# Four half steps moved and a norm rebalanced in a seven-stage attention kernel

## The reference

```
L0: y = norm(x + attention(x, x, causal)), lengths taken from the scores   a0
    y = norm(y + attention(y, ctx))                                        a1
    x = norm(y + relu(y W1 + b1) W2 + b2)            width 256             f0
L1: x = x + attention(rms(x), rms(x), mask) Wo                             a2
    x = x + attention(rms(x), ctx, mask) Wo                                a3
    x = x + mixture of 8 experts, top 2, and a shared one                  moe
L2: the same two attentions with biases and layer norms, then              a4 a5
    x = norm(x + relu(x W1 + b1) W2 + b2)            width 1024            f2
L3: out = norm(x + attention(x, ctx, causal)) * gamma + beta, 8 heads      a6
```

## Time and profile before

| | us |
|---|---|
| runs shown | 2715.59, 2716.20, 2718.04; median 2716.2 |
| profiled execution, its own time | 2713.54 |
| its span | 2711.2 |
| mean granted TensorE clock | 0.961 |

### The profile page before, as it was taken

The page is one execution under the profiler, slowest core; times in us unless marked ns, Lnnn a source line. Parts: engine busy times, 40 slices in busy tenths (PEclk is TensorE's granted clock), DMA queues, the critical chain, the costliest instruction groups (busy, mean ns, idle before and its releaser), DMA issues. The chain is left out here.

```text
span 2711.2 us, 44385 instructions
## 1 busy us (share of the span) xinstructions
PE 2493.1 (92%) x16014; PEld 1367.7 (50%) x16014; DVE 1770.2 (65%) x4316; ACT 1402.3 (52%) x1969; POOL 750.9 (28%) x915
## 2 busy tenths in 40 slices
PE   6999998989999999997999998799999999797896
PEld 3544433333444434443999998334434443385553
DVE  3566777677666676774457774577777777455554
ACT  1555565555555555555348875155555555452332
POOL 2244434443321111101016564202222112223012
PEclk7999999999999999998899999699999999998998
DMA  5222222122223223220127885423322322001331
GB/s 169 60 52 72 58 62 64 37 65 53 56 80 108 64 73 92 73 53 20 44 82 217 223 220 125 125 64 85 103 67 71 94 69 65 3 8 40 84 85 41
DMA packets 102213, 218.55 MB, mean 81 GB/s; under 512 B 19116, under 2 KB 35372, under 8 KB 100716
## 3 DMA queue, kind: packets, MB, share of 16 engines
q1 hardware_dynamic: 93164, 203.66, 27.8%
q0 software_dynamic: 8832, 12.06, 2.3%
HBM read 100.34 MB, written 12.58 MB: 42 GB/s over the span
## 5 line engine op out<-in xcount | busy, mean ns | idle before, releaser
L1150 ACT ACTIVATE probT_a<-scores 128x1024 f32<-128x1024 f32 (+3 forms) x832 | 779.3, 947 | 696.1 <-PE scores L981 422.6
L1265 DVE CUSTOM_DVE_ANT_0 ring<-ring,maskb_a 128x512 f32<-128x512 f32 x1024 | 686.3, 716 | 186.9 <-PE ring L999 177.6
L999 PE MATMUL ring<-stacks_a 64*128 64x512 f32 (+7 forms) x1664 | 465.2, 458 | 60.3 <-DVE negm_a L1263 24.4
L1020 PE MATMUL outputs<-probT_a,V_a 128*32 128x512 f32 (+6 forms) x3328 | 441.6, 574 | 12.3 <-ACT oT_a L1159 8.3
L1263 DVE TENSOR_REDUCE negm_a<-ring 128x1 f32<-128x512 f32 (+3 forms) x640 | 331.5, 564 | 152.1 <-PE ring L1005 110.4
L999 PEld LDWEIGHTS ring<-stacks_a 64*128 64x128 f32 (+1 forms) x1664 | 207.6, 189 | 381.0 <-issue 139.4
L960 PE MATMUL scores<-stacks_a 64*128 64x512 f32 (+7 forms) x1664 | 392.3, 444 | 2.5 <-DMA stacks_a<-narrow_a 2.5
L960 PEld LDWEIGHTS scores<-stacks_a 64*128 64x128 f32 (+1 forms) x1664 | 167.8, 185 | 241.9 <-issue 156.0
L909 POOL TENSOR_SCALAR maskb_a<-ints_a 128x1024 bf16<-128x1024 int32 x31 | 112.9, 3641 | 385.8 <-DMA ints_a<-in_mask 290.9
L981 PE MATMUL scores<-maskT_a,identb 64*64 64x512 bf16 x1024 | 210.2, 401 | 0.0
L981 PE MATMUL scores<-swapped_a,identb 64*64 64x512 bf16 x1024 | 206.8, 401 | 0.0
(11 more groups left out here) (243 smaller groups left out, 3760.7 us busy)
## 6 DMA issues: line engine op xcount, KB each, us to landing
stacks_a<-parts_a SPq DMA_DIRECT2D x672, 128.0 KB
raw<-in_moew SPq DMA_DIRECT2D x92, 512.0 KB, 4.1
ints_a<-in_mask SPq DMA_DIRECT2D x31, 512.0 KB, 3.7
swapped_a<-maskT_a SPq DMA_DIRECT2D x32, 256.0 KB, 3.6
wt<-in_w SPq DMA_DIRECT2D x7, 1024.0 KB, 4.9
kvT_a<-in_ctxT SPq DMA_DIRECT2D x12, 512.0 KB, 3.4
wrow<-in_row SPq DMA_DIRECT2D x7, 512.0 KB, 5.8
stacks_a<-narrow_a SPq DMA_DIRECT2D x224, 8.0 KB
```

The source lines that it names most:

```text
L999: last = pe.matmul(bank("S", j, n, e)[:, 0:w], Q[rows, g, qt * P:(qt + 1) * P], K[rows, g, 0:w], start=True, stop=not a.causal)
L1020: last = pe.matmul(OB[x * slot:(x + 1) * slot, q0:S], V[:, m % 2, kb, c:c + slot], probT[:, kb % 2, x, q0:S], start=(kb == 0), stop=(kb == ...
L1150: act.activation(probT[:, kb % 2, 2 * p:2 * p + 2, q0:S], scores_bank(j, n)[:, :, q0:S], ACT.Exp, bias=0.0, scale=-1.0).then_inc(c_exp.sem, 1)
L1265: least = dve.tensor_tensor_reduce(sc, sc, maskb[:, m % 2, qt, :], 1.0, BIG * 2, ALU.add, ALU.min, out)
```

## The change

- In the table: "q" part 1 of the next unit in a0 and a1 from half step 9 to 8; "tokens" from 18 to 17 (to 16 for a stage on the context with rms norm, a3), "norms" from 21 to 19 (a3: 20); the second "fh" from 17 to 16.
- In L3 a new flag `apart` holds: "root" is issued with "on", "ln" two half steps after "on"; POOL forms `shift` as well, and ACT centres instead of DVE.
- The last unit of L3 gets its gain and bias on DVE instead of POOL.
- Each batch's output leaves in two transfers of two tiles.
- `schedule` is rewritten with an inner function; the order of the list that it gives for a given table is the same.

```diff
+        self.apart = self.spaced or dk == 32
@@ timetable
         if a.spaced:
             out += [(2 + t, "root", -1, qt), (5 + t, "ln", -1, qt)]
+        elif a.apart:
+            out += [(2 + t, "root", -1, qt), (4 + t, "ln", -1, qt)]
         else:
             out += [(t + (5 if a.wo else 3), "root", -1, qt), (t + (5 if a.wo else 3), "ln", -1, qt)]
...
-    out += [(h + 1, "q", 1, 1), (h + 3 if a.length else h + 2 * step, "k", 1, 1), (2 * h + 1, "V", 1, 0), (2 * h + 2 * step, "V", 1, 1)]
+    out += [(h if a.length else h + 1, "q", 1, 1), (h + 3 if a.length else h + 2 * step, "k", 1, 1), (2 * h + 1, "V", 1, 0), (2 * h + 2 * step, "V", 1, 1)]
...
-    out += [(2 * h, "cnld", 2, 0), (2 * h + step, "tokens", 2, 0),
-            (2 * h + 5 * step // 2, "norms", 2, 0),
+    out += [(2 * h, "cnld", 2, 0), (2 * h + (0 if a.kv == "ctx" else step // 2), "tokens", 2, 0),
+            (2 * h + (4 if a.kv == "ctx" else 3) * step // 2, "norms", 2, 0),
...
-    out += [(13, "fx", -1, 0), (14, "fx", -1, 1), (15, "fh", -1, 0), (17, "fh", -1, 1)]
+    out += [(13, "fx", -1, 0), (14, "fx", -1, 1), (15, "fh", -1, 0), (16, "fh", -1, 1)]
@@ sync
-                if kind == "ln" and last and n == QT - 1:
+                if kind == "ln" and last and n % 2 == 1:
                     _, b, _, _ = stage_of(j)
-                    for t in range(QT):
+                    for t in range(n - 1, n + 1):
                         sp.wait_ge(*c_done.at(j, t))
-                    sp.dma_start(io["out"][b:b + 1, :, :].rearrange("o (q p) d -> p (o q) d", p=P),
-                                 X[:, b * QT:(b + 1) * QT, :]).then_inc(c_out.sem, 16)
+                    sp.dma_start(io["out"][b:b + 1, (n - 1) * P:(n + 1) * P, :].rearrange("o (q p) d -> p (o q) d", p=P),
+                                 X[:, b * QT + n - 1:b * QT + n + 1, :]).then_inc(c_out.sem, 16)
@@ gpsimd
-                    if a.spaced or kind == "froot":
+                    if a.apart or kind == "froot":
...
+                    if last_unit(j):
+                        continue
                     pool.wait_ge(*c_centred.at(*key))
@@ scalar
-                if kind == "fl" or (kind == "ln" and att[units[j][0]].spaced):
+                if kind == "fl" or (kind == "ln" and att[units[j][0]].apart):
@@ vector
-                if kind == "ln" and not a.spaced:
+                if kind == "ln" and last_unit(j):
+                    r = n % 2
+                    dve.wait_ge(*c_centred.at(j, n))
+                    dve.tensor_tensor(xh[:, r, :], xh[:, r, :], wrow[:, k, 2, :], ALU.mult)
+                    dve.drain()
+                    dve.tensor_tensor(tile(b, n), xh[:, r, :], wrow[:, k, 3, :], ALU.add).then_inc(c_done.sem, 1)
+                if kind == "ln" and not a.apart:
```

More of the change, by code:

```diff
@@ L207, in schedule, with besides @@
                 beside.setdefault(t, []).append((st, work, ahead, n))
[L208 to L215, removed]
+        def besides(h):
+            found = []
             for of, work, ahead, n in beside.get(u * halves + h, []):
@@ L218, in schedule @@
                     if of == stages[0] and there(4 * m + n):
-                        yield (work, 4 * m + n, 0)
+                        found.append((work, 4 * m + n, 0))
                     continue
@@ L226, in schedule @@
                     if st == of and wanted(work, ATT[int(st[1:])], st, b):
-                        yield (work, k, n)
+                        found.append((work, k, n))
             if m == base and len(units) > 1:
@@ L231, in schedule @@
                     if u * halves + h == t * halves // 8 and wanted(work, a, *units[1]):
-                        yield (work, base + 1, n)
+                        found.append((work, base + 1, n))
+            return found
+        masked = there(j) and ATT[int(units[m - base][0][1:])].mask is not None
+        for h in range(halves):
+            first = h - h % couples
+            if not masked:
+                turns = (("ST", h), ("S", h), ("exp", h))
+            elif h == first:
+                turns = (("S", h), ("ST", h), ("exp", h))
+            else:
+                turns = (("ST", h), ("exp", h), ("S", h))
+            for kind, n in turns:
+                if kind == "S" and there(j + 2):
+                    yield (kind, j + 2, n)
+                if kind != "S" and there(j):
+                    yield (kind, j, n)
+            yield from besides(h)
             kb = h // couples - 1
@@ L541, in attention_block, with last_unit @@
         work = list(schedule(stages, base))
+        def last_unit(j):
+            return last and j + 1 == base + len(units)
         def two_before(tally, *key):
@@ L621, in attention_block @@
                 x_done[(*units[j], n)] = c_done.at(j, n)
-                if last and n == QT - 1:
-                    c_out.mark(j)
+                if last and n % 2 == 1:
+                    c_out.mark(j, n)
             if kind == "fl":
```

## The result

| | us |
|---|---|
| runs of the changed kernel | 2674.53, 2678.45, 2688.00; median 2678.45 |
| profiled execution, its own time; its span | 2674.53; 2672.6 |
| mean granted TensorE clock | 0.970 (before 0.961) |
| ratio to before | 0.987, 95% interval 0.9845 to 0.9895 |

The kernel got 37.7 us faster by the medians. The forecast was 21.7 us, with a range that ended at 2684. A second set of four runs of the same kernel, beside twelve of before, gave 2678.7 and a ratio of 0.9866 (0.9852 to 0.9881).

What follows compares the result with a forecast made beforehand. PE, busy for 92% of the span, was taken as the bound, with gains from its idle time and clock. 4.7 + 0.3 + 1.6 + 6.9 + 3.3 + 1.8 + 3.1 = 21.7 us off 2716.2 gave 2694.5, range 2684 to 2708.

Steps and rivals of the forecast that it cites:

- norms: 4.7: Half steps 22 and 23 of eight units: moving "norms" earlier removes PE's stall, 4.7 us, between 2 and 5.6.
- The sign that the prediction named: Half steps 22 and 23: no PE wait over 0.7 us there would show the forecast right.
- q: 1.6 at full clock: Half steps 8 and 9: q fills PE's wait, 0.4 per a1 unit, 0.1 per a0 unit; 1.6 us, between -2 and +3.
- The slower rival: Half step 8 of seven units: q starts late, delays the minima, each unit gets a low stretch; 2728 us, chance 0.05.
- The clock in L0 and L1: 6.9: L0 and L1: low-clock stretches net 4.3 fewer at 1.6 us each, 6.9 us, between 0 and 11.2.
- seven lose their cause: Half steps 8, 9, 22, 23: seven low stretches lose the wait before them; 3/4 counted gone, one new.
- tokens and fh: 0.3: "tokens" in L0 goes where PE works on V, 0.3 us, between 0 and 0.7; "fh" at 16, zero.
- L3 between units: 3.3: Half steps 2 to 5, three times: DVE loses centrings and a wait for POOL's root, 3 x 1.1 = 3.3 us.
- the case that the prediction priced at 2700: L3: by the skill's SBUF rule POOL blocks all 16 y of DVE, 7.0 us in place of 1.2.
- L3's clock: 1.8: L3 between units: two of three stretches had a low clock; 55% of 2 x 1.6 is 1.8 us, between 0 and 3.2.
- The end: 3.1: Last unit of L3: SP issues earlier and the last transfer is half as large, 3.1 us, between 1.5 and 4.4.
- The rival "the clock falls elsewhere": L0, L1 and L3: low stretches come as often at other places, so the sum lacks 6.9 + 1.8; 2703 us, chance 0.21.

Runs made afterwards that it cites:

- tokens_fh: Kernel before with "tokens" and the second "fh" moved as in the change, "norms" left in its old half steps: 2706.45 us, ratio 0.9973.
- l3_alone: Changed kernel with its table entries for L0 and L1 put back, so only the L3 and output parts stay: 2705.71 us, ratio 0.9976 to before.
- q_alone: Kernel before with only part 1 of the next unit's "q" moved from half step 9 to 8 in a0 and a1: 2701.48 us, ratio 0.9955.
- norms_alone: Kernel before with "norms", "tokens" and the second "fh" moved as in the change, q and L3 left: 2694.05 us, ratio 0.9935.
- warm_scores: Kernel before with the key score matmul pair issued twice in half steps 6 to 9, 22 and 23 of the first nine units: 2702.61 us, ratio 0.9949.

## Why the prediction was wrong, point by point

- **norms: 4.7, the step that failed first.** "In a2 it is 0.53, and nothing in a3's third unit" was PE's idle time in the earlier trace rows, the length less the busy column. The lengths stood beside it: 4.60 with the norms' stall, 3.60 without. Their difference, 1.0, was the answer (1.09 measured), and the busy column, 4.07 against 3.60, held the other half: the first matmul of a split pair. Five units make 5.4 us, not 2.5. In the units beside f0 the idle time was right where it was read: at full clock a1's unit 2 took 5.8 us in half steps 22 and 23 and now takes 4.4, the 1.4 of the forecast. The 0.6 estimated for the first unit of a2 was too small: 6.3 us there with the stall (tokens_fh, no low stretch), 4.9 without. No stall came to half step 20 in a2 and a3. The sign that the prediction named, no PE wait over 0.7 us, came in: the largest in half steps 22 and 23 of a1's unit 2 is 0.57 us.
- **q: 1.6 at full clock.** In a0 0.1 a unit was forecast; half steps 8 and 9 fell from 6.2 to 5.5 where no low clock disturbs the comparison. This is no split pair: the busy column is the same (4.73 and 4.68), and PE's idle time fell, from 1.5 to 0.8 us. The prediction had this fall, and a larger one, to 0.4, in its term for the clock; for the length it followed DVE's instructions alone and came to 0.1. In a1's unit 1 idle time fell from 2.0 to 1.1, where 0.4 of length was forecast. In unit 0 of a0 the move cost 0.5 us (3.8 to 4.3 in half steps 8 and 9), where 0.1 of gain was counted. The slower rival did not come: q starts where the prediction put it.
- **The clock in L0 and L1: 6.9, the largest miss of the profiled pair.** 1.6 us a stretch was near for half step 9 (8.9 and 7.2 us in a1's last unit, before and l3_alone) and high elsewhere: 0.8 in half step 23 of a1's unit 2, 1.3 in the mean over the changed code. The count was wrong: 4.3 fewer were forecast. In lengths of 3.4 us before's code had 11 and 9 in two profiles and the changed one 0 to 3 in six, so 6 to 11 fewer, an estimated 8 to 14 us. By the same price some 9 of the 23.7 us of the nine units are not clock, where the terms for q, norms and tokens had 4.1. Over several profiles these misread waits, 5 us here and 2.9 in a2 and a3, weigh at least as much as the clock. The failed step is "seven lose their cause": I let the stretches in half steps 7 and 13, and in half step 9 of a1's last unit and a2's first, stay as if each had its own wait and no other. But q_alone, which touches no stall at 22 and 23, left 3 of 11 in all, and norms_alone 5. By these counts less idle time in a unit lowered the chance of a low stretch anywhere in it, though before's own code lost three of its 11 in l3_alone. Why one particular stretch came or went is not settled.
- **tokens and fh: 0.3.** 1.2 of their own at least.
- **L3 between units: 3.3.** Right. With no low clock on either side, 15.84 us (warm_scores, which is before's code in L3) went to 14.58 twice, and 11.77 to 11.00: 3.3 in all. y of tile 2 did not wait for L1193. DVE's y did lie beside POOL's gain, once in each of the three stretches: 0.84 us instead of 0.43, so 0.4 a stretch where 0.25 was taken off. The other 13 of L3's 16 took 0.42 to 0.43, and the case that the prediction priced at 2700 did not come.
- **L3's clock: 1.8.** One of the two stretches went in the profiled run, 1.35 us; both in l3_alone.
- **The end: 3.1.** 3.8 in the profile; no y was stretched beside POOL.
- **The start: 0.** 3.8 us of the profiled difference can't be laid to the change: kernels without filler there started at 63.8 to 70.0 us in eleven profiles, before's code at both ends, by where its low stretches fall.
- **The rival "the clock falls elsewhere"** did not come, and the slower one neither. The rule of the Trainium skill (TensorE: Matmul & The Clock Gate, Part 1), a gate that runs freely so that the same kernel shows different cold counts, is borne out for the count: 0 to 3 in one code. I had held against it that three runs agreed within 0.1%; twelve runs of before then spread over 2708.8 to 2716.2. As a reason for a smaller gain it failed, since the mean count followed PE's idle time.
- **The range** failed because every misread term erred to the same side. I had spread them as if independent.

## What to carry to other kernels

Take what a stall costs from the length of the same half steps with and without it, not from idle time alone: a matmul that should have run beside its twin hides in the busy column. Where low stretches lie behind short waits, as here, a wait that goes is worth its length and a share of the low stretches of the whole neighbourhood; count them over several profiles before and after. Work without use in PE's waits can pay for itself, if it is no longer than the wait.

## What was not expected of the hardware

- 108 matmuls more made the kernel before 13.8 us faster by the medians.
- Two matmuls of 64 rows, 128x512 in fp32, were through in 0.43 us when issued together and held PE for 1.08 when DVE's bank releases split them.
- POOL waited 3.6 us for one transfer of a mask half in one profile and 5.1 in another, and the later one made DVE wait 1.7 us.
